# Window attention: heads turned by row and column tiles, queries and keys moved by DMA, TensorE's program without a loop

## The reference, cut to what matters

```python
h = layernorm(xf, norm1_g, norm1_b)            # tokens in windows of 8 x 8
qkv = h @ qkv_w.T + qkv_b                      # 4 heads of 12 channels
q, k, v = (qkv[0] * scale, qkv[1], qkv[2])
attn = einsum('whnd,whmd->whnm', q, k) + bias  # 64 x 64 per window and head
attn = softmax(attn)
o = einsum('whnm,whmd->whnd', attn, v)
xf = shortcut + o @ proj_w.T + proj_b
m = gelu(layernorm(xf, norm2_g, norm2_b) @ fc1_w.T + fc1_b) @ fc2_w.T + fc2_b
xf = xf + m
```

## Time and profile before

| | |
|---|---|
| median of 3 runs | 1855.17 us (1854.99 to 1858.85) |
| the profiled execution, its time and span | 1855.03 us, 1853.2 us |
| busy over the span | PE 96%, DVE 84%, ACT 68%, POOL 35% |
| attention | from about 29 us (first transpose of `xn`) to 772 us (last store of `mid`) |
| MLP, then convolution | the rest |

### The profile page before, as it was taken

How to read it: one execution, slowest core, us unless ns; L and a number is a source line. 1 busy time by engine, 2 the same in 40 slices (tenths; PEclk the granted TensorE clock), 3 DMA queues, 4 the chain that set the end, 5 groups by cost and what they waited for, 6 DMA issues and landing times.

```text
span 1853.2 us, 75137 instructions
## 1 busy us (share of the span) xinstructions
PE 1780.5 (96%) x30472; PEld 1535.5 (83%) x30472; DVE 1561.9 (84%) x2842; ACT 1253.0 (68%) x2790; POOL 646.1 (35%) x867
## 2 busy tenths in 40 slices
PE   5999999999999999599999899999999999999997
PEld 4888888888888888455555799999999999999997
DVE  4999999999999999678888778778878777777786
ACT  2788888888888887467777556656566566566563
POOL 4333333333333333421220533535335353444240
PEclk9999999999999999799999999999999999999999
DMA  2222222222222222388986444546364564545441
GB/s 67 67 75 76 78 74 74 74 76 78 74 74 74 76 79 73 93 196 212 207 201 154 106 99 132 121 103 154 89 150 105 117 145 103 112 133 110 102 124 36
DMA packets 286439, 198.85 MB, mean 107 GB/s; under 512 B 225991, under 2 KB 275672, under 8 KB 276504
## 3 DMA queue, kind: packets, MB, share of 16 engines
q1 hardware_dynamic: 282114, 189.12, 39.9%
q0 software_dynamic: 2368, 6.25, 1.6%
q10 hardware_dynamic: 1750, 0.39, 0.1%
HBM read 128.36 MB, written 54.72 MB: 99 GB/s over the span
## 4 chain that ended last, share of the span: by engine, by line
PE 53%; DMA 2%; DVE 1%; issue 1%; ACT 0%; ACTq 0%; SPq 0%; DVEq 0%
PE psum L1152 15%; PE psum L1171 14%; PE psum L1206 9%; PE psum L1195 5%; PE psum L682 3%; PE psum L673 3%; PE psum L663 2%; PE psum L687 2%; DMA img_mid<-room 1%; PE psum L701 1%; DVE room L737 0%; DVE room L750 0%; DMA room<-in_fc_wT 0%; ACTq L763 0%; DVE room L913 0%
## 5 line engine op out<-in xcount | busy, mean ns | idle before, releaser
L962 POOL TENSOR_TENSOR mats<-mats,dscale 112x2048 f32<-112x2048 f32 x72 | 260.9, 3624 | 279.8 <-DMA mats<-in_taps 277.0
L912 ACT ACTIVATE room<-psum 64x512 f32<-64x512 f32 (+1 forms) x336 | 177.9, 530 | 254.1 <-PE psum L1171 248.8
L1152 PE MATMUL psum<-ew,xp 64*100 64x96 f32 x6144 | 314.9, 251 | 8.8 <-issue 4.2
L1152 PEld LDWEIGHTS psum<-ew,xp 64*100 64x100 f32 x6144 | 291.2, 165 | 15.4 <-issue 7.8
L913 DVE TENSOR_SCALAR h<-psum 100x384 f32<-100x384 f32 x384 | 209.6, 556 | 71.5 <-PE psum L1152 47.8
L913 DVE TENSOR_SCALAR room<-psum 64x512 f32<-64x512 f32 (+1 forms) x336 | 207.5, 618 | 68.9 <-PE psum L1171 62.2
L1171 PE MATMUL psum<-h,mats 101*64 101x128 f32 x4608 | 260.5, 273 | 0.7 <-DVE h L913 0.7
L1171 PEld LDWEIGHTS psum<-h,mats 101*64 101x64 f32 x4608 | 252.8, 137 | 5.2 <-issue 1.1
L344 PE MATMUL psum<-kb,qa 128*64 128x256 f32 x2048 | 244.6, 381 | 0.6 <-DVE prob L443 0.6
L912 ACT ACTIVATE h<-psum 100x384 f32<-100x384 f32 x384 | 188.3, 491 | 61.5 <-PE psum L1152 45.6
L344 PEld LDWEIGHTS psum<-kb,qa 128*64 128x64 f32 x2048 | 140.8, 138 | 56.3 <-issue 1.9
(11 more groups left out here) (161 smaller groups left out, 3314.1 us busy)
## 6 DMA issues: line engine op xcount, KB each, us to landing
mats<-in_taps SPq DMA_DIRECT2D x69, 896.0 KB, 6.2
tok_mid<-mid SPq DMA_DIRECT2D x128, 224.0 KB, 1.9
room<-tok_mid SPq DMA_DIRECT2D x64, 448.0 KB, 5.6
piece<-img_mid SPq DMA_DIRECT2D x196, 63.8 KB, 2.4
img_mid<-room SPq DMA_DIRECT2D x128, 97.5 KB, 3.7
kb<-kk SPq DMA_DIRECT2D x512, 24.0 KB
out<-yc SPq DMA_DIRECT2D x32, 384.0 KB, 4.4
scratch<-in_x_tokens SPq DMA_DIRECT2D x126, 96.0 KB, 1.9
```

Of the source, the lines that this page charges most:

```text
L912: return nc.scalar.activation(dst, src, ACT.Relu)
L962: nc.gpsimd.tensor_tensor(m, m, bc(scale[0:MROWS, at:at + TCH], 2, POUT), ALU.mult).then_inc(mats_scaled, 1)
L1152: mm = nc.tensor.matmul(psum[0:PIN, bank_of(j + u), p:4 * CH:4], xp[hx][rows, 2 * j + p, :], w1[rows, c, :], start=True, stop=True)
```

## The change

- Everything turned by PE is turned in halves of 64 rows, each half on its own row tile and with its own PSUM bank; the copies by ACT put the halves together. The output projection goes by windows on column tiles. v comes out with the heads of one parity on 64 partitions, so that ACT copies it in two parts.
- PE's order in a step becomes: turn `on`, turn `xn`, turn all probabilities, qk, projection, v, probabilities times v, all scores of group i+1. Its program is written out for all steps.
- PSUM banks are assigned anew, and waits keep ACT and DVE from reading a bank while PE writes it (the qk copy waits for v, the v copy for `o`).
- ACT copies queries and keys together into `qk`. `kb` has its columns by head, window, key. SP moves the keys by four DMAs with rows of 2 KB and the queries by a fifth, and it does so at the head of its step, before the store of `mid`.
- DVE no longer copies queries and no longer centres; POOL multiplies the sums by 1/48 (`mean`, `mean2`) and subtracts. DVE's order changes too.
- The projection's weights are laid out on the host with heads of 16 rows (HEAD) and its bias in row 12 of the first head; `on` has the same layout.

```diff
-        kk = [sb(f"kk{s}", [P, TOK]) for s in range(2)]
-        kb = [sb(f"kb{s}", [P, 2 * PAIRS, NH, NT]) for s in range(2)]
+        qk = [sb(f"qk{s}", [P, TOK]) for s in range(2)]
+        kb = [sb(f"kb{s}", [P, NH, 2 * PAIRS, NT]) for s in range(2)]
...
-        ps_k = psum[:, 4:6, 0:TOK // 2]
-        ps_a, ps_b = psum[:, 6, :], psum[:, 7, :]
-        ps_xT, ps_v, ps_y = ps_a[:, 0:TOK // 2], ps_a[:, 0:PAIRS * C], ps_a[:, TOK // 2:TOK // 2 + PAIRS * C]
-        ps_o, ps_oT = ps_b[:, 0:PAIRS * NH * VE], ps_b[:, TOK // 2:TOK]
+        ps_xT, ps_oT, ps_o = psum[:, 4:6, 0:P], psum[:, 4:6, P:2 * P], psum[:, 4:6, 2 * P:2 * P + PAIRS * NH * VE // 2]
+        ps_k = psum[:, 6:8, 0:TOK // 2]
+        ps_y, ps_v = (psum[:, bank, TOK // 2:TOK // 2 + PAIRS * C] for bank in (6, 7))
...
 # SP
+                if has(i + 2):
+                    sp.wait_ge(qk_copied, i + 3)
+                    for h in range(NH):
+                        r = slice(ONE + HD * h, ONE + HD * h + HD)
+                        sp.dma_start(kb[s][r, h, :, :].rearrange("q n m -> q (n m)"), qk[s][r, :]).then_inc(heads_put[s], 16)
+                    sp.dma_start(qa[s][ONE:ONE + C, :], qk[s][0:C, :]).then_inc(heads_put[s], 16)
                 if has(i - 3):
                     sp.wait_ge(mid_done, i - 2)
                     sp.dma_start(d["tok_mid"][i - 3], mid[1 - s][:, :, :]).then_inc(stored[1 - s], 16)
-                if has(i + 2):
-                    sp.wait_ge(k_copied, i + 3)
-                    for h in range(NH):
-                        r = slice(ONE + HD * h, ONE + HD * h + HD)
-                        sp.dma_start(kb[s][r, :, h, :], kk[s][r, :].rearrange("q (n m) -> q n m", m=NT))\
-                            .then_inc(keys_put[s], 16)
...
 # PE
-            def turn_probs(i, s, k):
-
-                for p in range(PAIRS // 2 * k, PAIRS // 2 * (k + 1)):
+            def turn_probs(s):
+
+                for p in range(PAIRS):
                     for h in range(2):
-                        at = 256 * (p % 2) + P * h
-                        mm = nc.tensor.transpose(ps_p[:, k, at:at + P], prob[1 - s][:, NH * p + 2 * h:NH * p + 2 * h + 2, :],
-                                                 ident[:, :])
+                        at = NT * (2 * p + h)
+                        for w in range(2):
+                            r = slice(NT * w, NT * w + NT)
+                            mm = nc.tensor.transpose(ps_p[:, w, at:at + NT], prob[s][r, NH * p + 2 * h:NH * p + 2 * h + 2, :],
+                                                     ident[r, r])
                 mm.then_inc(pT_ready, 1)
...
+                if has(i - 2):
+                    pe.wait_ge(oT_copied, i - 1)
+                    wait(pe, qk_copied, min(i + 2, GROUPS) if isinstance(i, int) else i + 2)
+                    wait(pe, res_done, i - 2)
+                    for a in range(PAIRS // 2):
+                        for w in range(2):
+                            mm = nc.tensor.matmul(ps_y[NT * w:NT * w + NT, 2 * C * a:2 * C * a + 2 * C],
+                                                  oT[:, P * a + NT * w:P * a + NT * w + NT], w_o[:, :], start=True, stop=True)
+                    mm.then_inc(y_ready, 1)
+                if has(i + 1):
+                    for a in range(PAIRS // 2):
+                        for w in range(2):
+                            at = PAIRS * C // 2 * w + 2 * HD * NH // 2 * a
+                            for h in range(2):
+                                mm = nc.tensor.matmul(ps_v[NT * h:NT * h + NT, at:at + 2 * HD * NH // 2],
+                                                      xnT[1 - s][:, P * a + NT * w:P * a + NT * w + NT], v_part(h),
+                                                      start=True, stop=True)
+                    mm.then_inc(v_ready, 1)
...
-            schedule(pe, step, lambda pe: pe.wait_ge(bias_put, 4), -1)
+            for i in range(-4, GROUPS + 3):
+                if i == -1:
+                    pe.wait_ge(bias_put, 4)
+                step(i, i % 2)
...
 # ACT, whose step is now: xnT, oT, probT twice, qk, lnv, rstd, Exp of the scores, v twice
+                    act.wait_ge(qk_ready, i + 3)
+                    if has(i + 1):
+                        act.wait_ge(v_ready, i + 2)
+                    if has(i):
+                        act.wait_ge(heads_put[s], heads_of(i, s))
+                    nc.scalar.activation(halves(qk[s][0:ONE + C, :]),
+                                         ps_k[0:ONE + C, :, :].rearrange("q e (a t) -> q e a t", t=P), ACT.Copy)\
+                        .then_inc(qk_copied, 1)
...
+                if has(i + 1):
+                    act.wait_ge(v_ready, i + 2)
+                    if has(i - 1):
+                        act.wait_ge(o_ready, i)
+                    for h in range(2):
+                        r = slice(NT * h, NT * h + NT)
+                        last = nc.scalar.activation(
+                            vb[1 - s][r, :, :, :, VE * h:VE * h + HD].rearrange("q p k w e -> q w (p k) e"),
+                            ps_v[r, :].rearrange("q (w x e) -> q w x e", w=2, e=HD), ACT.Copy)
+                    last.then_inc(v_copied, 1)
...
 # POOL
                 if has(i - 3):
+                    pool.wait_ge(sum2_done, i - 2)
+                    nc.gpsimd.tensor_tensor(mean2[:, :], sums2[1 - s][:, :], per_c[:, :], ALU.mult).then_inc(mean2_done, 1)
+                    pool.wait_ge(mean2_done, i - 2)
+                    nc.gpsimd.tensor_tensor(cen2[1 - s][:, :, :], mid[1 - s][:, :, X_AT[1 - s]:X_AT[1 - s] + C],
+                                            bc(mean2[:, :], 2, C), ALU.subtract).then_inc(cen2_done, 1)
...
                 if has(i + 4):
+                    pool.wait_ge(sum_done, i + 5)
+                    nc.gpsimd.tensor_tensor(mean[:, :], sums[s][:, :], per_c[:, :], ALU.mult).then_inc(mean_done, 1)
+                    pool.wait_ge(mean_done, i + 5)
+                    nc.gpsimd.tensor_tensor(cen[s][:, :, :], x_of(i + 4), bc(mean[:, :], 2, C), ALU.subtract).then_inc(cen_done, 1)
```

More of the change, by code:

```diff
@@ L43 @@
 VE = HD + 1
+HEAD = 16
 MID = 112
@@ L159, in attention @@
         rden = sb("rden", [P, PAIRS * NH])
-        on = sb("on", [P, PAIRS, ONE])
+        mean, mean2, per_c = (sb(n, [P, PAIRS]) for n in ("mean", "meanb", "per_c"))
+        on = sb("on", [P, PAIRS * NH, HEAD])
         oT = sb("oT", [P, TOK // 2])
@@ L386, in step @@
                     mm.then_inc(qk_ready, 1)
-                elif has(i):
+                elif has(i + 1):
                     pe.wait_ge(v_copied, i + 1)
+                if has(i - 2):
+                    pe.wait_ge(oT_copied, i - 1)
+                    wait(pe, qk_copied, min(i + 2, GROUPS) if isinstance(i, int) else i + 2)
+                    wait(pe, res_done, i - 2)
+                    for a in range(PAIRS // 2):
+                        for w in range(2):
+                            mm = nc.tensor.matmul(ps_y[NT * w:NT * w + NT, 2 * C * a:2 * C * a + 2 * C],
+                                                  oT[:, P * a + NT * w:P * a + NT * w + NT], w_o[:, :], start=True, stop=True)
+                    mm.then_inc(y_ready, 1)
@@ L398, in step @@
                     mm.then_inc(o_ready, 1)
-                if has(i + 1):
-                    wait(pe, res_done, i - 1)
-                    for a in range(PAIRS // 2):
-                        for w in range(2):
-                            mm = nc.tensor.matmul(ps_v[NT * w:NT * w + NT, 2 * C * a:2 * C * a + 2 * C],
-                                                  xnT[1 - s][:, P * a + NT * w:P * a + NT * w + NT], w_v[:, :],
-                                                  start=True, stop=True)
-                    mm.then_inc(v_ready, 1)
@@ L447, in step @@
                     dve.wait_ge(y_ready, i - 1)
+                    if has(i + 2):
+                        dve.wait_ge(qk_copied, i + 3)
                     wait(dve, stored[s], 8 * (i - 2 - s))
@@ L468, in step @@
             def step(i, s):
-                def turned_probs(k):
-                    act.wait_ge(pT_ready, 2 * i - 1 + k)
-                    nc.scalar.activation(probT[:, 2 * k:2 * k + 2, :, :].rearrange("q p h n -> q (p h n)"), ps_p[:, k, :], ACT.Copy)\
-                        .then_inc(pT_copied, 1)
-                if has(i):
-                    act.wait_ge(v_ready, i + 1)
-                    v = ps_v.rearrange("q (b h e) -> q b h e", h=2, e=HD)
-                    for h in range(2):
-                        for w in range(2):
-                            dst = vb[s][NT * h:NT * h + NT, :, :, w, VE * h:VE * h + HD].rearrange("q p k e -> q (p k) e")
-                            last = nc.scalar.activation(dst, v[NT * w:NT * w + NT, :, h, :], ACT.Copy)
-                    last.then_inc(v_copied, 1)
+                if has(i + 2):
+                    act.wait_ge(xnT_ready, i + 3)
```

(16 more changed lines are left out.)

151 lines of the change are left out of this document (62 added, 89 removed).

## The result

| | median | runs | ratio to before, 95% interval |
|---|---|---|---|
| before | 1857.01 us (1854.99 to 1859.16) | 4 | |
| after | 1933.36 us (1921.17 to 1949.2) | 4 | 1.0405 (1.0353 to 1.0458) |

The forecast was 1779 us and a range of 1755 to 1830; 0.07 was given to slower. The profiled execution of after took 1934.09 us, its span 1932.2.

A forecast was written before the change was run, and what follows sets the result against it. PE was taken as the bound at 5.63 us a step, DVE next at 5.49. A step of 5.05 saves 0.58, 72 us over 124 steps; with 2 to 4 at the ends, 76: from 1855.17 to 1779 us, range 1755 to 1830.

The forecast's parts named there:

- PE's work: PE's matmuls and transposes in one attention step: 4.89 us with tiling changes, in a step of 5.05 in place of 5.63.
- half transposes: PE's turning in attention: 24 halves run as 12 pairs at 0.055 us, 0.66 in place of 1.32 a step.
- Rival C: PE's half transposes not cheap at 128 columns: 1843 us if pairs overlap (chance 0.03), 2010 us if nothing does (0.03).
- v copies: ACT's copies of v: four of 96 columns become two of 192, 0.33 us each, 0.66 for 1.00 a step.
- copy of 112 rows: ACT's joint copy of queries and keys: same 512 columns as with 48 rows, so 0.593 us.
- new wait for xnT: PE ahead of qk waits for ACT's copy of the turned `xn`: 0.17 us a step, not there today.
- The price of the longer code: PE's program written out for all steps: put at nothing, as the MLP's written-out matmuls run without gaps.
- 5s+1.11: SP's queue per step: five transfers between SBUF tiles at one price each, plus 1.11 us for store and x load; 4.3 us.
- The size of s: Issue price on SP's queue of one transfer between SBUF tiles: taken as 0.63 us, between bounds 0.36 and 0.83.
- rival B: SP's queue is the bound: 1805 us at an issue price of 0.83, 1915 at 1.0; chance 0.09 up to 0.89, 0.04 beyond.
- The small product: POOL's two products of four columns in attention: 0.11 us taken, between 0.11 and 0.508.
- the walk's own T: Length of one steady attention step from walking all engines' queues: 5.05 us, in place of 5.63.

The follow-up runs named there:

- looped kernel: The changed kernel (after) with PE's program put back in the loop of two steps: 1866.57 us, ratio 1.0046 to before.
- loop_mid4_rows16: After with PE's program back in its loop, four buffers of `mid` in place of two, and key transfers of 16 rows (queries 64): 1812.66 us, ratio 0.9799.
- flat_mid4_rows16: After, PE's program still written out, with four buffers of `mid` and key transfers of 16 rows (queries 64): 1820.33 us, ratio 0.981.
- others_flat: After with PE's program in its loop and the programs of SP, DVE, ACT and POOL written out: 1859.15 us, ratio 1.0005.

## Why the prediction was wrong

**What held.** PE's work: a step without waits is 5.17 to 5.18 us against 5.05. The half transposes are cheap, though not as cheap as read from the earlier trace rows: the starts of eight pairs lie 0.0626 us apart (0.44 for the seven distances between them), in place of 0.055; twelve pairs are 0.75 in place of 0.66, though the wait for xnT hides the probabilities' share of that. v is 0.45 (0.48), output projection 0.38 (0.36), qk 0.63 and scores 1.86 (1.73 + 0.13). Rival C is out, and with it the load rule of the Trainium skill (page "TensorE: Matmul & The Clock Gate", section "LDWEIGHTS (loading the stationary operand)") for this form: by it all turning would take 2.6 us, and all of it, with the entry into qk, takes 0.94 from start to start. The v copies took 0.326 us (0.33), the copy of 112 rows 0.597 (0.593). The new wait for xnT was there, some 0.12 us (0.17): in after, qk starts 0.05 us behind the end of ACT's copy, 0.642 us after the first turned probability, while looped steps in which the probabilities start late have as little as 0.523.

**The step that failed first: "The price of the longer code I put at nothing too: the MLP's code is written out and its matmuls follow one another without gaps".** It looked for the price at PE, and PE pays nothing that I can measure (a step without waits is 5.17, and without the loop it even saves the 0.08). Its program is fetched by packets of 16 KB, 13 or 14 in 100 us, that hold up other DMAs, and who waits for those pays: 67 of the 76 us by which after is slower than before, as long as the store is late as well. With slack for the transfers the same packets cost 8. Nothing in the trace of before would have given the 67, but its page has the queue: 171 packets and 2.80 MB on "q8 instruction" (after: 269 and 4.41), nearly none of them in attention.

**The second: the order on SP's queue.** I summed the queue (5s+1.11) and walked the heads to their landing, and did not walk the store, which the change moved behind five issues. Its reader is DVE's wait on `stored`, from an issue that comes 4.4 us later relative to the keys. With the measured lengths: issue at 3.95 us, landing 2.1 later = 6.05, wanted one step after the qk copy = 5.2 and a little. The looped kernel shows this alone: its mean step is 5.72 in place of the 5.28 of loop_mid4_rows16, and four buffers of `mid` take back 29.5 us, 16 rows 34, both 54. The two steps do not add: of the 154 us between the forecast and the measured time, the loop alone takes back 67 and slack alone (flat_mid4_rows16) 113, both together 121.

**The size of s.** Taken as 0.63, measured 0.775 for the 12-row transfers and 0.54 for the queries (to the store 0.81). 5s is 3.95, and 5s+1.11 is 5.06: rival B in its own form, the sum of the queue, did not decide. Its late issues did. The price goes mostly by rows: 12 rows 0.775, and with eight pieces a row 0.83; 16 rows 0.61. The rule on the semaphore's increments (the Trainium skill, page "DMA: Bandwidth & Descriptors", section "Why a DMA increments its semaphore by 16 and not by 1") spoke against my 0.63, for it sets transfers whose rows divide over fewer than 16 engines apart. The trace agrees that the 12-row form is the dear one; why, no run shows.

**POOL.** The small product took 0.20 us in place of 0.11, with 0.18 of wait behind it. Between 200 and 600 us no engine waited for POOL.

**With both faults mended** (loop_mid4_rows16) the change gains 43 us against before on the same chip, 1812.7 in place of the 1779 forecast. The rest of the gap is 34 us, and the mean step, 5.28 in place of 5.05, makes up 29 of them: 0.05 a step up to the start of qk (0.94 in place of 0.89), 0.09 from there to the next step (4.25 in place of 4.16), and 0.08 for PE's loop, which the kernel as changed does not have. The last 5 us lie within what the rest of the kernel varies by (1076 to 1088 us).

**Slips in the sums.** By the walk's own T, rival B at s = 1.0 would be 1911 us in place of 1915, and rival C 1840 and 2003 in place of 1843 and 2010; the chances outside the range sum to 0.12 in place of 0.14. The forecast does not rest on these.

## What to carry to other kernels

When a DMA is moved on a queue, walk its own landing to whoever waits for it, buffer reuse included, and look at what it waits for itself: a queue in order makes everything behind it wait for that too. Before writing out a loop, look at which transfers land with little to spare. The fetched code cost nothing measurable to the engine that runs it, but it made stores land up to 2.4 us late (4.5 in place of 2.1), and each reader without that much slack pays. Slack (a deeper ring of buffers, an issue that is cheaper because it has 16 rows) took back more here than either order of the same transfers on one queue.

## What the runs showed of the hardware that I had not expected

- PE's written-out program comes in packets of 16 KB, 0.9 to 1.8 us each, one in 7.4 us on average in this stage; that of the other four engines in packets of 8 KB, 0.3 to 0.76 us, on another queue. Stores with a packet of either kind beside them can land late (up to 4.5 us in after, 3.2 in others_flat); of those without one, none took over 2.13 and 2.39.
- All 28 of SP's issues over 1 us in after overlap such a 16 KB packet; plain data in packets of 16 KB made landings late (2.0 to 2.5 us) but no issue.
- A transfer of one row of 16 KB was cut into 16 packets of 1 KB; two rows with a gap went as packets of 16 KB.
- One DMA a step of 64 bytes within the chip's memory made the stores behind it land 1.3 us later than one of 16 KB did.
